# Routing steps of eight images and the loads of an expert stage, put in another order (one core, Trainium2)

## The reference

```python
x = x + cross_attention(layernorm(x), ctx, ctx, tau, delta)      # layer 0
x = x + encoder_block(layernorm(x))                              # layer 1, below
x = x + cross_attention(layernorm(x), ctx, ctx, tau, delta)      # layer 2
x = x + sets_of_experts(layernorm(x))                            # layer 3

# encoder_block(x): self-attention over 256 tokens, then one expert of 8 for each token
hn = layernorm(x, ln1_g, ln1_b)
x = x + (softmax(q @ k.T / 4) @ v) @ wo + bo
hn2 = layernorm(x, ln2_g, ln2_b).reshape(-1, 256)
idx = argmax(hn2 @ gate_w + gate_b)                              # 2048 tokens, 8 experts
y = relu(hn2 @ w1[e] + b1[e]) @ w2[e] + b2[e]                    # for e = idx of the token
return x + y
```

## Time and profile before

| | us |
|---|---|
| median of 3 runs | 963.87 |
| lowest and highest | 962.43, 969.52 |
| the profiled execution | 966.02 |
| its span on the core | 964.2 |
| TensorE busy | 786.9 (82%) |
| VectorE busy | 507.2 (53%) |
| ScalarE busy | 344.5 (36%) |
| GpSimd busy | 242.9 (25%) |

### The profile page before, as it was taken

One profiled execution on the slowest core, in us unless ns is written; L12 is line 12 of the kernel. 1 busy time (PEld: TensorE's weight loads), 2 busy tenths in 40 slices (PEclk: granted clock), 3 DMA queues, 4 the chain that ended last, 5 costly groups with the idle time before them and its releaser, 6 DMA issues.

```text
span 964.2 us, 16230 instructions
## 1 busy us (share of the span) xinstructions
PE 786.9 (82%) x6103; PEld 597.1 (62%) x6103; DVE 507.2 (53%) x1223; ACT 344.5 (36%) x627; POOL 242.9 (25%) x242
## 2 busy tenths in 40 slices
PE   3557989899999999951499999956369898997898
PEld 3345666566666666531499999944246666675775
DVE  4544577876688676223112112224555788345495
ACT  2224544435354544510122222203124464443313
POOL 2422333322233231112211111014523442211100
PEclk9768988989999999965699999987677799755899
DMA  4949464754454665336544556425938252060202
GB/s 158 125 66 193 80 92 66 104 79 71 71 115 78 69 129 159 111 109 70 195 166 169 189 189 169 154 73 74 134 47 113 46 89 58 13 274 6 91 1 88
DMA packets 66896, 103.29 MB, mean 107 GB/s; under 512 B 21614, under 2 KB 56942, under 8 KB 61662
## 3 DMA queue, kind: packets, MB, share of 16 engines
q1 hardware_dynamic: 64403, 97.07, 47.9%
q0 software_dynamic: 2416, 5.19, 2.9%
HBM read 56.61 MB, written 7.28 MB: 66 GB/s over the span
## 4 chain that ended last, share of the span: by engine, by line
PE 61%; DVE 13%; DMA 8%; ACT 5%; issue 5%; POOL 4%; SPq 4%; DVEq 0%; POOLq 0%; ACTq 0%
PE PS L723 9%; PE U L734 8%; PE U L640 8%; PE MB L573 6%; PE MB L661 5%; PE PS L626 4%; PE MB L651 4%; PE MB L603 4%; DVE R L1262 3%; PE MB L589 3%; SPq L1459 2%; DMA y<-yb,pos 2%; DMA QKa<-mTa 2%; DVE nma L1071 2%; PE MB L813 2%
## 5 line engine op out<-in xcount | busy, mean ns | idle before, releaser
L1071 DVE TENSOR_REDUCE nma<-MB 128x2 f32<-128x512 f32 (+1 forms) x192 | 124.3, 673 | 43.9 <-PE MB L603 43.5
L899 ACT ACTIVATE Pa<-PS 128x1024 f32<-128x1024 f32 (+1 forms) x96 | 97.5, 1023 | 73.1 <-PE PS L626 72.1
L1304 POOL TENSOR_TENSOR mv<-mv,vec 128x2 f32<-128x2 f32 x48 | 34.7, 723 | 272.0 <-DVE mv L1026 271.8
L603 PE MATMUL MB<-QKa 99*128 99x120 bf16 (+1 forms) x512 | 75.1, 265 | 26.9 <-DVE nma L1071 14.2
L640 PE MATMUL U<-Pa,Vaa 128*32 128x256 f32 (+1 forms) x768 | 92.4, 405 | 0.9 <-ACT Pa L899 0.7
L723 PE MATMUL PS<-mzT,mw 128*128 128x128 f32 x736 | 87.8, 278 | 1.8 <-ACT mzT L920 1.8
L723 PEld LDWEIGHTS PS<-mzT,mw 128*128 128x128 f32 x736 | 85.7, 195 | 2.4 <-issue 2.3
L734 PE MATMUL U<-mw,mdT 128*128 x368 | 83.3, 379 | 2.3 <-DVE mdT L1210 2.3
L603 PEld LDWEIGHTS MB<-QKa 99*128 99x128 bf16 x512 | 41.3, 107 | 60.4 <-DVE nma L1071 22.1
L734 PEld LDWEIGHTS U<-mw,mdT 128*128 128x128 f32 x368 | 68.2, 190 | 11.0 <-issue 2.7
L1218 DVE TENSOR_TENSOR yt<-U,mb 128x256 f32<-128x256 f32 x23 | 9.8, 425 | 123.2 <-PE U L734 123.2
(11 more groups left out here) (194 smaller groups left out, 1424.6 us busy)
## 6 DMA issues: line engine op xcount, KB each, us to landing
mw<-in_mw SPq DMA_DIRECT2D x31, 1024.0 KB, 5.7
QKa<-spa SPq DMA_DIRECT2D x144, 128.0 KB, 5.2
Qb<-spb SPq DMA_DIRECT2D x48, 128.0 KB, 5.1
Oa<-Uba SPq DMA_DIRECT2D x16, 256.0 KB
v<-in_v SPq DMA_DIRECT2D x1, 4096.0 KB, 13.6
v<-in_v SPq DMA_DIRECT2D x4, 1024.0 KB, 11.4
W<-in_W SPq DMA_DIRECT2D x3, 1280.0 KB, 7.4
yb<-yt SPq DMA_DIRECT2D x23, 128.0 KB, 1.7
```

The source lines that it names most:

```text
L603: i = e.matmul(b[:, keys * j:keys * j + keys], Q[0:99, h0 + j, 128 * qt:128 * qt + 128], K[0:99, h0 + j, 0:keys], start=True, stop=True)
L899: e.activation(p[0:keys, :], ps[0:keys, :], ACT.Exp, scale=0.25).then_inc(sems["exp"], 1)
L1071: e.tensor_reduce(A.nm[qt][:, h0:h0 + heads], b[:, 0:heads * keys].rearrange("p (h s) -> p h s", h=heads), AX.X, ALU.max, negate=True).the ...
L1304: e.tensor_tensor(rs[r][:, 0:2], ve[r][:, 0:2], mhalf[:, 0:2], ALU.pow).then_inc(sems["rs"], 1)
```

## The change

The diff in full:

```diff
-T_AFTER = (2.1, 2.35, 2.67, 2.85, 3.35, 3.45)
+T_AFTER = (1.75, 2.0, 2.2, 2.35, 2.6, 2.7)
...
-T_WEIGHTS = (13.3, 13.5, 14.1, 14.3, 15.1, 15.3, 15.6)
+T_WEIGHTS = (13.3, 13.5, 14.1, 14.3, 15.1, 15.3, 16.05)
...
         if L == 1:
-            task(at(T_AFTER), [("na", n, 2), ("xy", n)], [("nb", n, 2), ("hs", n)], [("gt", n)], [("gl", n)], [("gr", n)],
+            task(at(T_AFTER), [("xy", n), ("na", n, 2)], [("nb", n, 2), ("hs", n)], [("gt", n)], [("gl", n)], [("gr", n)],
                  [("gs", n)])
...
         def table():
 
+            tile_weights(0)
+            g.wait_ge("d_i", 16)
+            tile_weights(1)
+
             g.wait_ge("p2", 16)
             g.wait_ge("offset", 16)
             e.dma_start(b2[:, :, :], D["b2"]).then_inc(sems["d_b2"], 16)
-            for j in range(3):
-                tile_weights(j)
+            tile_weights(2)
```

## The result

| | before | after |
|---|---|---|
| median, us | 965.38 (962.43 to 973.02, 9 runs) | 957.55 (955.31 to 960.75, 9 runs) |
| ratio, 95% interval | 1 | 0.9914 [0.9889, 0.994] |
| profiled execution, its span | 966.02, 964.2 | 960.75, 958.6 |
| end of the attention (U of image 15) | 412.67 | 413.92 |
| first expert matmul | 470.79 | 462.96 |

The changed kernel takes 0.86% less, where 1.5% (14.2 us) was forecast: it lies within the 1% that the text called "same". Applied to the 963.87 from which the forecast counted, the ratio gives 955.6: inside the range of 944 to 957.5, near its slow end, and nearer to rival (a)'s 955.2 than to the 949.7 that was predicted. In the profiles the first expert matmul comes 7.8 us earlier, at the low end of the forecast's own bounds of 7.4 to 17.2, and the span is 5.6 us shorter, outside them.

A forecast was written before the change was run, and what follows sets the result against it. After the second attention, one thread from image 15's outputs to the first expert tile bounds the kernel. 7.1 + 0.3 + 2.8 + 3.6 + 1.9 - 1.5 = 14.2 us off the 963.87 median gives 949.7; range 944 to 957.5.

The forecast's parts named there:

- rival (a): In the tail only the order pays; scatters and gather stay as slow whatever runs beside them: 955.2 us, chance 0.15.
- the first three terms: From attention's end to normed y: reciprocal 7.1 us earlier, projection 0.3, residual to normed y 2.8; together 10.2 us gained.
- the transfers: Image 15's scatters, the table's gather and the first rows' gather before the first expert tile: 3.6 + 1.9 - 1.5 us.
- O's turning, 2.4 us: After the attention, image 15's O lands 2.4 us after issue with mw2 behind it; reciprocal 7.1 us earlier.
- The scatters, 3.6: Image 15's two scatters land 9.2 us after the first issue instead of 12.8, as most loads wait: 3.6 us gained.
- the pair from 381.5: Earlier scatters whose second landed 8.9 us after the first issue; nearest row and lower bound for image 15's scatters.
- The table's gather, 1.9: After the scatters, the gather into ids takes 3.9 us instead of 5.8 with fewer loads beside it: 1.9 us gained.
- The first rows' gather, -1.5: The gather into zt takes 4.2 us instead of 2.7, with 3 MB of loads sent beside it: 1.5 us lost.
- The rule: DMA engines serve queues in turn, so small transfers lose nothing to loads; last three terms 0, sum 10.2 us.
- Rival (b): Clock stays at 2.4 GHz over the pause, halving image 15's sums and projection: 3.6 us more gained, 946.1, chance 0.1.
- Rival (c): Attention loses more than the tail wins: up to 974.2 us; chance 0.06 slower by over 1%, 0.09 loss within 1%.
- Rival (d): In the attention, keys arrive late behind the scatters: 0.8 us for one image, at most 3 for all; no chance given.

The follow-up runs named there:

- (c) alone: The kernel before with only the last two mw2 blocks issued behind image 15's turning of O: 957.97 us, ratio 0.9923.

## Why the prediction was right, and where it was wrong

**The side and the first three terms were right.** 7.1 + 0.3 + 2.8 = 10.2 was forecast for order and queue; the profile shows 6.4 + 0.1 to 0.3 + 2.6, some 9.2, and (c) alone shows whose the largest is. The number itself is in the range partly by luck: of 14.2 us the two medians show 7.8, and the 4.0 of the transfers came to nothing. That is the outcome of rival (a), held at 0.15, though not its mechanism, since both gathers moved.

**O's turning, 2.4 us, was mis-sized at 3.57.** The 2.4 was right for a queue with nothing ahead (2.36 in (c) alone; the slices of the earlier trace rows end one earlier than the text counted, at 329.6, which changes nothing). The step that failed is "what the turning takes with nothing ahead": in the new order image 14's `hs` stands ahead of O, a move that the order on SyncE shows and that the sum left out. I had counted only what moved behind. "The gate, not the DMA, is what ends last" was wrong with it: the chain goes through the DMA. With the hb write later O lands after 2.35, and there the gate does end last, 4.12 after the end where the forecast said 4.2.

**The scatters, 3.6, were 1.8.** The step that failed is "I take 9.2, by the nearer row". The pair from 381.5 took 8.9, but image 15's pair never came under 10.76 up to the gather, even with idle DMA engines. I read 12.8 as 9 of the scatters' own and 4 of loads; it is about 10.8, and 2 that image 14's scatters and the loads share. The prediction named image 14's second scatter as still under way and gave it no term; by the comparison of old and new steps the larger part of the 2 goes with it, though no run isolates it. Rival (a) had right that most of the time is the scatters' own; its "against", the pair from 381.5, misled me. What sets apart that pair, and image 14's pairs of 8.4 to 9.7 in the tail, stays open; I did not try it.

**The table's gather, 1.9, was right to a tenth**: 5.82 to 3.89, and 3.15 with no load at all. Rival (a) had said it wouldn't move.

**The first rows' gather, -1.5, was -3.8.** The mechanism was right and stood in the prediction: SyncE wakes at the same landing as the thread and sends 3 MB beside the gather. The size was outside its own bounds of 0 to 2.8, since the row it came from was a gather beside one load, and here it is three. Delaying the loads by one landing takes all of it away (2.71). With this the three terms of the transfers, 4.0 together, came to about nothing, and the wait alone to 2.3 us of loss by its ratio (0.0024 x 965, with an interval of 0.2 to 4.4). That the small transfers gain more than the first rows lose is the step on which the size of the forecast failed: 14.2 less 4.0 is 10.2, and the profile shows 9.2 less what follows.

**The rule.** In this case the table's gather takes 3.1 to 3.2 with nothing beside it, 3.7 to 4.4 beside the rest of one load, 5.8 to 6.7 beside several; the first rows' 2.7 to 2.8 alone and 5.3 to 7.0 beside three or four loads. Small transfers are slowed to about twice, but not put last behind 3 MB. That agrees with queues served in turn, as the Trainium skill has it in "DMA: Bandwidth & Descriptors", section "Queues, rings and completion order". What I drew from it ahead of the rivals, that small transfers lose nothing to loads when the queues take turns, didn't follow: beside loads they took 2 to 4 us more here. That the wait brought nothing has another reason, the first rows' gather.

**The clock.** Rival (b), the clock at 2.4 GHz over the pause, didn't come: the sums take 3.68 and the projection 3.72 in after, as before (3.67, 3.52), and the granted clock reads 0.50 from 418 to 426 us.

**The other side.** Rival (c), a loss in the attention, didn't come: TensorE is busy 25.00 of 25 us from 350 on, and the end is 1.25 later, below the 2 us that I set. Its reverse came in two kernels, 158.8 and 160.2 instead of 164.4, by a change of 0.05 in one due time: between kernels that are else alike in the attention the place of the gate's logits was worth 2.5 us (160.2 against 162.7 with the hb write late) and 5.4 us (158.8 against 164.2 with the late wait), and I had costed the steps' places at nothing. Rival (d), late keys, isn't seen: among TensorE's waits of after from 200 to 412 us none is for a DMA.

**Behind the first expert matmul** after takes 2.2 us more than before (495.6 against 493.4), though nothing was changed there. 0.9 is in the first tile: its first group of 32 matmuls takes 6.38 instead of 5.48 and the second 3.81 in both, at a granted clock that rises within the first, and later in after. These are the stretches from 3.2 to 5.2 us behind the group's start in before, and from 3.0 to 5.0 in after (the clock is the third number from the end):

```profile
474.00:476.00 2.00, 2.00 (x19) 2.00 (x19) 0.00 (x0) 0.00 (x0) 0.00 (x0) 0.93 0.00 0
...
466.00:468.00 2.00, 2.00 (x12) 2.00 (x11) 0.00 (x0) 0.00 (x0) 0.00 (x0) 0.50 0.18 66
```

Over all kernels this first group took 5.2 to 6.5 us, and all from the first expert matmul to the end of the span 493 to 496. Whether the later rise comes from the loads or from where in time the tile falls isn't settled: the kernels with the shortest group (5.18 to 5.48) send their loads early, but the one with the old loads and the new steps took 6.08. The rest of the 2.2 us I did not look for.

## What to carry to other kernels

Before a load is made to wait, ask who else wakes at the landing that it waits for: a wait that ends together with the thread's own next small transfer puts the loads exactly beside that one, and waiting one landing longer cost nothing that the rows show and gave back 2.7 us of transfers. Ahead of a small transfer on the critical thread count every DMA of its queue, those that move there with other steps too: two blocks of 1 MB ahead cost 7.4 us here and 256 KB 1.2 to 2.1. If scatters of one image are still under way when the next one's are sent, they add up, as two more added 10.3 us here: look for them before blaming the loads. And take a slow transfer's own time from a run or a stretch with idle DMA engines before calling it contention.

## What the hardware showed that I had not expected

- Two scatters of 128 four-byte elements into memory take 10.76 us with nothing else under way, during which the DMA share reads 0.00 and 0 GB/s; two more right behind them add 10.3 us. An idle share can be a transfer under way. Earlier pairs took less, down to 8.4, and why isn't shown.
- A gather of the first rows took 2.7 to 2.8 us alone, 5.3 to 7.0 beside 3 or 4 MB of loads.
- A 256 KB write into memory, issued 2.3 us ahead in the same queue, delays a turning DMA of 256 KB from 2.35 to between 3.57 and 4.42.
- A load sent beside the scatters moved 38 to 88 GB/s until about their landing, and 378 to 391 after. The low rate at a high share of the earlier trace rows is the same in before: the first `mw1` load up to the last scatter's landing at 459.2. It looks as if here the scatters held up the load more than it held up them, but no run isolates it, and it isn't always so: in before b2 moves 227 to 365 GB/s from 446.4 us to 449, while image 14's second scatter lands only at 453.2, and beside the pair from 381.67 a load moved at up to 492 GB/s.
- A due time moved by 0.05 of an image shortened the attention from image 8's sums on to 158.8 and 160.2 us, where the kernels without it lay from 162.6 to 164.6, with no instruction added or removed.
